# Cross-attention and a mixture of experts: GpSimd's instructions of 512 columns cut in two and in four

## The reference

```
x   : 16 x 256 x 256,  ctx : 16 x 77 x 256      (float32)
x = x + attention(layernorm(x), ctx, ctx)        16 heads of 16, softmax over 77 keys
h = layernorm(x)
p = softmax(h @ router_w);  the two largest of 8 experts, weights p
x = x + sum over the two of  p_e * (silu(h @ gate_w[e]) * (h @ up_w[e])) @ down_w[e]
```

## Time and profile before

| | |
|---|---|
| median of 3 runs | 913.49 us (912.96 to 916.47) |
| the profiled execution's own time | 915.49 us |
| its span, first to last instruction | 913.7 us |
| mean granted TensorE clock | 0.986 |
| busy: PE, PEld | 94%, 86% |
| busy: DVE, ACT, POOL | 67%, 52%, 31% |
| GpSimd instructions | 343 |

### The profile page before, as it was taken

How to read it: one execution, slowest core, us unless ns; L and a number is a source line. 1 busy time by engine, 2 the same in 40 slices (tenths; PEclk the granted TensorE clock), 3 DMA queues, 4 the chain that set the end, 5 groups by cost and what they waited for, 6 DMA issues and landing times.

```text
span 913.7 us, 32215 instructions
## 1 busy us (share of the span) xinstructions
PE 855.9 (94%) x12208; PEld 784.6 (86%) x12208; DVE 613.3 (67%) x1932; ACT 479.3 (52%) x900; POOL 286.1 (31%) x343
## 2 busy tenths in 40 slices
PE   4788999999999998899999999999999999999995
PEld 3676877777777787899999999999999999999995
DVE  7788899888998868575575466457546657454442
ACT  5666887888888866353353344225334435223231
POOL 4767444334444245322122221222112221222112
PEclk9999999999999979999999999999999999999998
DMA  6211232222322453663262145224324422221121
GB/s 217 81 43 43 69 97 79 71 81 68 97 74 71 127 158 96 178 167 72 60 154 56 24 98 135 35 59 118 80 59 95 110 53 36 35 35 29 31 35 18
DMA packets 72885, 74.04 MB, mean 81 GB/s; under 512 B 20749, under 2 KB 62811, under 8 KB 72827
## 3 DMA queue, kind: packets, MB, share of 16 engines
q1 hardware_dynamic: 46906, 36.08, 13.8%
q0 software_dynamic: 13536, 19.85, 12.2%
q10 hardware_dynamic: 12384, 17.35, 6.0%
HBM read 45.18 MB, written 26.80 MB: 79 GB/s over the span
## 4 chain that ended last, share of the span: by engine, by line
PE 67%; ACT 4%; DVE 4%; issue 3%; DMA 1%; POOL 0%; ACTq 0%; DVEq 0%; POOLq 0%; SPq 0%
PE bank L555 15%; PE bank L557 14%; PE bank L556 14%; PE bank L759 6%; PE bank L761 6%; PE bank L760 6%; PE bank L733 2%; PE bank L624 1%; PE bank L631 1%; ACT pt_hi L884 1%; ACT probs L878 1%; ACT xn L919 1%; DMA raw<-expert_rows 1%; DVE h_lo L1443 0%; ACT h_hi L953 0%
## 5 line engine op out<-in xcount | busy, mean ns | idle before, releaser
L555 PE MATMUL bank<-xg,e_hi 128*128 128x128 f16 x2176 | 373.8, 220 | 1.4 <-DVE xg L1413 1.3
L557 PE MATMUL bank<-xg,e_lo 128*128 128x128 f16 x2176 | 373.9, 220 | 0.0
L556 PE MATMUL bank<-xg,e_hi 128*128 128x128 f16 x2176 | 373.8, 220 | 0.0
L1660 POOL DMA_INDIRECT out<-y_sb,tok_row x67 | 108.0, 1612 | 434.2 <-DVE y_sb L1432 408.8
L555 PEld LDWEIGHTS bank<-xg,e_hi 128*128 128x128 f16 x2176 | 213.5, 98 | 3.4 <-DVE xg L1413 1.8
L556 PEld LDWEIGHTS bank<-xg,e_hi 128*128 128x128 f16 x2176 | 213.5, 98 | 0.7
L557 PEld LDWEIGHTS bank<-xg,e_lo 128*128 128x128 f16 x2176 | 213.6, 98 | 0.0
L948 ACT ACTIVATE g_act<-bank 128x512 f32<-128x512 f32 x136 | 81.2, 597 | 232.3 <-PE bank L557 225.2
L1437 DVE SCALAR_TENSOR_TENSOR h_full<-bank,g_act 128x512 f32<-128x512 f32 x136 | 93.9, 690 | 115.2 <-ACT g_act L948 107.9
L759 PE MATMUL bank<-e_hi,h_hi 128*128 128x256 f16 x544 | 148.4, 273 | 3.4 <-DVE h_lo L1443 3.0
L760 PE MATMUL bank<-e_lo,h_hi 128*128 128x256 f16 x544 | 148.3, 273 | 0.0
(11 more groups left out here) (186 smaller groups left out, 1744.8 us busy)
## 6 DMA issues: line engine op xcount, KB each, us to landing
raw<-expert_rows SPq DMA_DIRECT2D x68, 132.5 KB, 2.5
e_stage<-in_gate_w ACTq DMA_DIRECT2D x24, 256.0 KB, 3.4
e_stage<-in_up_w ACTq DMA_DIRECT2D x22, 256.0 KB, 3.0
e_stage<-in_down_w ACTq DMA_DIRECT2D x20, 256.0 KB, 3.1
expert_rows<-pads SPq DMA_DIRECT2D x8, 530.0 KB
xin<-in_x SPq DMA_DIRECT2D x16, 256.0 KB, 2.8
xres<-in_x SPq DMA_DIRECT2D x16, 256.0 KB, 2.9
out<-x SPq DMA_DIRECT2D x16, 256.0 KB
```

What stands on the lines that cost most here:

```text
L555: pe.matmul(dst, a_hi(c), b_hi(c), start=c == 0, stop=False)
L556: pe.matmul(dst, a_hi(c), b_lo(c), start=False, stop=False)
L557: mm = pe.matmul(dst, a_lo(c), b_hi(c), start=False, stop=ends and c == chunks - 1)
L1660: pool.indirect_dma_start(out, bass.IndirectOffsetOnAxis(tok_from[:], 0), y_from[:], None, compute_op=ALU.add).then_inc(added, 16)
```

## The change

Each of the three instructions of an expert 0 piece becomes two of 256 columns, one right behind the other with no wait between them; only the second raises the semaphore. The subtraction of a batch's low rows, one instruction over 128 partitions, 2 tiles and 256 columns, becomes four of 128 columns each: for either half of the columns, one for either tile; only the last raises the semaphore. What is computed stays the same.

```
+SHORT = 2
 ...
                 for n in pieces:
-                    cols = slice(n * PIECE, (n + 1) * PIECE)
-                    pool.tensor_scalar(e_stage[:, cols], e_stage[:, cols], WS, None, ALU.mult).then_inc(e_scaled, 1)
+                    parts = [slice(at, at + PIECE // SHORT) for at in range(n * PIECE, (n + 1) * PIECE, PIECE // SHORT)]
+                    for cols in parts:
+                        ins = pool.tensor_scalar(e_stage[:, cols], e_stage[:, cols], WS, None, ALU.mult)
+                    ins.then_inc(e_scaled, 1)
                     pool.wait_ge(e_scaled, n + 1)
-                    pool.tensor_copy(e_hi[:, 0, cols], e_stage[:, cols]).then_inc(e_hi_ready, 1)
+                    for cols in parts:
+                        ins = pool.tensor_copy(e_hi[:, 0, cols], e_stage[:, cols])
+                    ins.then_inc(e_hi_ready, 1)
                     pool.wait_ge(e_hi_ready, n + 1)
-                    pool.tensor_tensor(e_lo[:, 0, cols], e_stage[:, cols], e_hi[:, 0, cols], ALU.subtract).then_inc(e_lo_ready, 1)
+                    for cols in parts:
+                        ins = pool.tensor_tensor(e_lo[:, 0, cols], e_stage[:, cols], e_hi[:, 0, cols], ALU.subtract)
+                    ins.then_inc(e_lo_ready, 1)
 ...
-                pool.tensor_tensor(parts[:, :, D:2 * D], x2n[:], parts[:, :, 0:D], ALU.subtract).then_inc(row_ready, 1)
+                for at in range(0, D, D // 2):
+                    for t in range(NT):
+                        ins = pool.tensor_tensor(parts[:, t, D + at:D + at + D // 2], x2n[:, t, at:at + D // 2],
+                                                 parts[:, t, at:at + D // 2], ALU.subtract)
+                ins.then_inc(row_ready, 1)
```

## The result

The changed kernel takes 909.98 us (median of 10 runs, 906.71 to 913.05), the kernel before 913.47 (10 runs, 910.35 to 917.33). The ratio is 0.9957, 95% interval 0.9942 to 0.9972: 0.4% faster, 3.5 us in the medians. The forecast was 909.9 us, inside a range of 906.5 to 915.0. The two profiled executions differ by more, 909.95 against 915.49, because that of before stood 2.0 us above its median and that of after on it: of their 5.5 us, the medians leave 3.5. So the profile of before is of an execution longer than most, and differences read against it may be too large by up to 2 us.

The account below looks back on a forecast made before the run. In attention's rounds that split expert 0, VectorE, delayed behind GpSimd's instructions, was taken as the engine others wait for. Expert 0's split -3.6 us, low rows 0, late keys hidden: from 913.49 to 909.9 us, range 906.5 to 915.0.

Parts of the forecast that it names:

- The late keys, part 3: Behind the third expert 0 stretch: k_diag spreads some 3 us late against 4.4 us free, so hidden, costing nothing.
- the shut seam: Rival at expert 0's halves: GpSimd enters the second half before VectorE gets in; +2.0 us, 915.5 us, chance 0.12.
- the rule that the prediction sets beside it: Skill's shared-port rule: the loser blocks for the whole instruction, L1576's 1.49 us; the sum would be some 1.5 us larger.
- How much of the waits goes: VectorE in the three expert 0 rounds: 5.6 us saved, 1.5 of new waits, net 4.1; 3.6 taken for the rounds.
- the 2.8 a round: VectorE's ln_tmp instructions in each of the three rounds: about 2.8 us forecast in place of 4.2 in the mean.
- the share of 0.8: Part of VectorE's waits that lengthens the three rounds: 8.0 of 10.3 us.
- What half an instruction costs: GpSimd's expert 0 halves: some 0.83, 0.39 and 0.66 us each; a piece 0.5 us longer, a stretch of four 2.0.
- The low rows: Four instructions at 0.43 us, +0.6 a batch, hidden in the loop; last batch 0, between -0.5 and +0.5 us.
- the three falls that the prediction names: TensorE's granted clock at its lower level, 0.57 at 42 to 46 and 86 to 90 us, the same at 59 to 63.
- the prediction's price of 0.7 a fall: One fall of TensorE's clock costs some 0.7 us, from the round after the last being 0.7 over.
- the clock comes back as well: Rival: shorter waits avert TensorE's clock falls around the three rounds, 2 us more, 907.5 us, chance 0.22.

Follow-up runs that it names:

- low rows only: The kernel before with only a batch's low-row subtraction in four instructions, expert 0's split whole: 911.9 us, ratio 0.9994.
- the memsets: The kernel before with expert 0's scaling, cast and subtraction each replaced by a write-only memset of 512 columns: 937.3 us on chip 2, ratio 0.9924.
- expert 0 only: The changed kernel with the low rows back in one instruction, so only expert 0's split is in halves: 909.8 us, ratio 0.9969.
- the scaling and cast alone: The kernel before with expert 0's scaling and cast in halves, subtraction and low rows whole: 942.8 us on chip 3, ratio 0.9972.
- whole instructions, spread: The kernel before with expert 0's twelve pieces placed over four rounds, every instruction whole: ratio 0.9967 on chip 2, 0.9973 on chip 3.
- the pieces spread: The changed kernel with expert 0's twelve pieces placed by a table over four rounds: 906.5 us, ratio 0.9933.
- the subtraction in halves: The kernel before with only expert 0's subtraction to e_lo in halves, scaling, cast and low rows whole: 907.7 us, ratio 0.9952.

## Why the prediction was right, point by point

**The total** came out as worked: -3.6 us expected, -3.5 measured. That it agrees to 0.1 us is luck. The waits were sized too small and the late keys were put at nothing, two errors of opposite sign, and they don't cancel to that figure either. Between the two profiled executions the three rounds are 7.6 us shorter, the two behind them 1.5 longer (20.45 and 19.54 in place of 19.61 and 18.87), and the rest of the kernel is 0.6 longer: 5.5 us less in all, of which 2.0 are the profiled execution of before standing above its median.

A second comparison tells how far the 7.6 can be trusted. The run with the low rows only differs from the changed kernel in expert 0's split alone and was profiled 0.3 us above its median. Against it the three rounds are 4.7 us shorter and the two behind them 2.5 longer, together the 2.2 us by which these two executions differ (912.15 and 909.95). So by these two comparisons the three rounds gain 4.7 to 7.6 us, and the lateness takes 1.5 to 2.5 back; nothing here narrows it further.

**VectorE waits for GpSimd's reads, and a wait ends at the seam:** shown, by the 23 instructions that all ended at a seam, by the memsets that hold no two-input instruction, and by expert 0 only. The rival of the shut seam is out. The reading that L1576 keeps such instructions out for its first 0.6 us only, against the rule that the prediction sets beside it, holds as well: all four that began in its first 0.4 us in the kernel before ended 0.62 to 0.63 us behind it, and L1124 at 75.71 in the changed one ended 0.41 us behind the start of a half, which lasts 0.84.

**How much of the waits goes:** sized too small. I counted 5.6 us saved less 1.5 of new waits, 4.1 net, of which 3.6 reach the rounds. By the estimate above the waits fell by 6.4 us (ln_tmp alone by 4.6, where the 2.8 a round forecast for it meant 4.3) and the three rounds by 7.6; in the second comparison it is 4.5 of waits and 4.7 of rounds. So both the 4.1 and the share of 0.8 were too low. The step that failed is the count of waits by the instruction that each ended with, as if all other phases stayed. The low rows alone took 2.4 us from the third round and the scaling and cast alone 6 from the three; both fit a kernel before that stood at a bad phase, where many small instructions began just behind the start of a long one. That is argued and not shown: the second figure compares chip 3 with chip 1 (whole instructions, spread, gave 64.49 and 63.03 on chips 2 and 3), and neither run is clear of no change in its total.

**What half an instruction costs:** right. 850, 400 and 670 ns against the estimates of 830, 390 and 660; two halves less one whole come to 0.21, 0.19 and 0.18 us. From one piece to the next it is 3.83 us (67.93 to 71.76) in place of 3.37 (72.87 to 76.24), 0.46 more against the 0.5 forecast. The low rows took 426 ns against 430.

**The late keys, part 3:** wrong. I took the earlier trace rows, 100.79, for the first use of the new keys and found 4.4 us of room. The first use is one unit earlier, behind the router's products, at 99.23: 2.9 us of room. My sum for the lateness doesn't hold as written either: 3.5 and 2.6 less 1.5 are 4.6 us, not 3. What was measured, counted from v_full: GpSimd came to the split of K 4.7 us later than before, SyncE took up 1.3 of it, the spreads began 3.4 us later (6.43 us in place of 3.01), and the keys landed some 3.6 later (14.2 in place of the 10.6 of my estimate). TensorE meanwhile was ready for them 1.1 us sooner (12.4 in place of 13.5), which left 1.8 us of room. So it stood 1.9 us, and the round behind the stretches was 1.9 us longer than with the pieces spread. "Hidden" should have been some 2 us off the gain. TensorE's clock then fell to its lower level (0.58 in the mean of 93 to 97 us), still in that round; the next one, whose own granted clock was 1.00, took 19.54 us where an even one is 18.9. From there on the even rounds are as before, 18.9 us.

**The low rows:** right. In the loop nobody waits for them. In the last batch h_lo took 0.97 us in place of the 1.67 of the earlier trace rows, and the transposes stood 0.9 us for the rows, nearly as forecast; from h_lo's start to x2t's end are 3.7 us against 3.8. Alone they make 0.9994.

**The clock.** Of the three falls that the prediction names, two lie in the second of the three rounds (0.84 in the rows above) and the third in the round behind them. The changed kernel had one fall in its three rounds, in the first (0.91), and one at 93 us. So the clock can be a part of the gain in the second round only: in the first the changed kernel was 1.7 us faster at the lower granted clock, and in the third 2.9 us faster at 1.00 in both. These two make 4.7 of the 7.6 us. In the second, 2.9 us, the prediction's price of 0.7 a fall would make it 1.4 for two, an estimate. Other runs agree that it is little: expert 0 only had falls at 53 and 80 us, and the subtraction in halves none before 318 and three rounds of 57.00 us, against the changed kernel's 57.21 with one fall. The rival *the clock comes back as well* is thus at most a smaller part, and the total, 3.5 us, asks for none of it.

## What to carry to other kernels

Where a small VectorE instruction takes several times its usual length and ends with one of GpSimd's, the two are tied, even with no semaphore between them; cut the longest two-input GpSimd instruction first, since a seam in it gave here as much as seams in all. Each seam costs its engine some 0.2 us, so look up who waits for GpSimd next, to the first reader and not the one after it, and place the work so that this one is in time. Waits of this kind depend on phase: a shift of one engine by 0.4 us took 1.3 us of waits from a round here. And look how far the profiled execution stands from the median before you price rounds with it: here that was 2.0 us, for a change of 3.5.

## What was not expected of the hardware

A memset of GpSimd's, which reads nothing, let every two-input VectorE instruction pass and still held the one-input L1102 on two to four elements for 0.27 to 0.40 us until its own end.

A GpSimd instruction of 1.49 us (L1576, which reads and writes 512 columns) kept two-input VectorE instructions out for its first 0.62 us only, while L1580 of 1.16 us and L1578 of 0.61 us kept them out to the end.

Three chips ran the same kernel at 912, 945 and 945 us; on the first the kernels profiled had a mean granted clock of 0.986 to 0.993 and even rounds of 18.9 us, on the other two 0.958 to 0.977 and 20 to 21 us.
